# Reordering a four-stage kernel's recurrence turns and their drain, and three repeated products of constants ahead of the experts

## The chip, the core and the metric

One core of a Trainium2 chip. The metric is the device time in microseconds (us), the median of the runs shown. TensorE is PE, VectorE is DVE, ScalarE is ACT, GpSimd is POOL and SyncE is SP.

## What is computed

```python
x = x + L0_attn(layernorm(x))     # two 64x64 states and a gated 64-vector, scanned over 4096 tokens
x = x + L0_ffn(layernorm(x))      # top-2 of 8 experts, 256 -> 1024 -> 256
x = x + L1_attn(x)[0]             # time mixing over tokens, channel mixing
x = x + L1_ffn(x)                 # gated 256 -> 1024 -> 1024 -> 1024 -> 256
```

The first line is where the change lies. For each token, with k, v, q, an importance i, a candidate nu and three shares p:

```python
pred = 0.5 * (q @ fH + q @ sH);  surprise = sigmoid(sum((v - pred)**2))
fH = a_f*fH + (1-a_f)*k(v - k@fH);  sH = a_s*sH + (1-a_s)*[i > 0.5]*k(v - k@sH)
ns = ns + [surprise > 0.7] * 0.1 * (nu - ns)
o  = p0*(q @ fH) + p1*(q @ sH) + p2*ns
```

Then o is scaled by its root mean square, goes through Wo and is added to x; x is normalised, and the router's logits choose two experts per token.

## The kernel before

The 4096 tokens are 32 chunks of 128, and 8 blocks b of four chunks. The recurrence is solved chunk by chunk in 16 **turns** u = 0 to 15 of two chunks each (j = 0, 1). Every engine has its own instruction order, written out by hand in `turn(u)`; semaphores tie them together, and an engine runs its instructions strictly in that order.

Within turn u PE runs eight **levels** n = 0 to 7 for the turn's own two chunks: `level` (lines 1168, 1169) squares the chunk's matrix and (line 1177) multiplies its right side. DVE's `apply(t, p, n)` (line 549) adds each product to the right side, ACT's `square` (lines 911, 914) takes the squares, and level n+1's product waits for `apply` of level n. Between the levels lie three other kinds of work:

- the **tail** for the two chunks of the turn before: PE's `y_transposes` (1185), `y_state` (1195) and `predict` (1201 to 1205), DVE's `rows_w` (556) and `new_state` (563 to 579). `new_state` first makes the new state (563) and then has six small instructions for the outputs (570 to 579, `pp_rdy` at 575);
- the **head** for the two chunks of the next turn: PE's `transposes` (1148, bank 4), ACT's `transposed` (902 to 904), PE's `grams` (1153, bank 4) and DVE's `masks` (535, 538), once for j = 0 around level 4 and once for j = 1 around level 7;
- the **stages of a block** that follow some turns behind: the neuron gates (590), `neuron_steps` and `neurons` (596, the scan at 601), `outputs` (611), `mean_squares` (617), `residual` (629), `stats` and `variances` (636, 641, 643), `norm` (647), ACT's `rows` (957) and `columns` (965), the logits (1229), `choose`, `gates`, `take_ranks` and `places` (662 to 697), and POOL's `scatter` (320), 8 indirect DMAs for a block. `at(u, parity, lag, stage)` runs a stage for block (u - lag)/2 in turns of that parity. Gates, ranks and places begin in turn 7, residuals in turn 4, stages of odd turns at lag 3 in turn 3.

Bank 4 holds the head's transposes and then its grams, for both chunks in turn. So PE's transposes of chunk j = 1 wait until DVE's masks have read the grams of j = 0:

```python
def transposes(t, p, j, bk=4):
    c = t * 2 + j
    pe.wait_ge(kq_rdy, c + 1)
    if c >= 2:
        pe.wait_ge(l_rdy, c)          # counted by masks()
```

They stand behind level 4 and `y_state(·, 1)` on PE; in odd turns `neuron_back` (1220) and the first `z1_columns` (1267) follow, then level 5.

After turn 15 comes the **drain**: the tail of turn 15 and the stages of blocks 5, 6 and 7, again in orders of their own. It ends with the scatters of blocks 6 and 7, 16 indirect DMAs one after another on POOL. Two of them stand ahead of the block end, six behind it. SP then waits for all rows, loads the first 256 rows of expert 0 (1446), PE transposes them (1516), DVE splits them (1640, 1642), and the experts' products begin (1413 to 1415).

Of the kernel before, what the change touches and what calls it, by code (L numbers as in the profile page):

```python
# [18 lines left out]
NC = S // CH  # L19
# [4 lines left out]
PJ = 3 * DS + 3  # L24
LOGIT = 0.8472978603872034
SQUARES = 5
LEVELS = SQUARES + 3
TT = 256
MIN_TILES = 2
# [45 lines left out]
def build(nc, A):  # L75
# [5 lines left out]
    with ctx:  # L81
# [34 lines left out]
        one_m = sb("one_m", [128, 128])  # L116
# [136 lines left out]
        def pj(o, n=1):  # L253
            return slice(o, o + n * DS)
# [48 lines left out]

        def bank_of(b, item):

            return (bank_behind if b == LAST else bank_in_turns)[item]


        def block_of(u, parity, lag):
# [70 lines left out]
        def _(dve):  # L380
# [175 lines left out]
                V.tensor_tensor(Wb[:, j, :].rearrange("p (m n) -> p m n", m=2), X[:, p, j, 0, :, :],  # L556
                                B[6][:, 256:384].rearrange("p (m n) -> p m n", m=2), ALU.subtract).then_inc(w_rdy, 1)

            def new_state(t, j):
                c = t * 2 + j  # L560
                dve.wait_ge(pp_ps, c + 1)
                for m in range(2):
                    last = V.scalar_tensor_tensor(state[half[m], m, :], state[half[m], m, :], alC[half[m], m:m + 1],
                                                  B[6][half[m], 384 + m * DS:384 + (m + 1) * DS], ALU.mult, ALU.add)
                last.then_inc(f_rdy, 1)

                k_, v_ = PR[:, c, pj(0)], PR[:, c, pj(DS)]
                by = lambda s_: small[:, s_, c:c + 1]
                from_fast, from_slow = B[6][:, 0:DS], B[6][:, DS:2 * DS]
                V.tensor_scalar(k_, from_fast, by(T0), None, ALU.mult).then_inc(po_st, 1)  # L570
                V.scalar_tensor_tensor(v_, from_fast, -0.5, v_, ALU.mult, ALU.add).then_inc(po_st, 1)
                dve.wait_ge(po_st, c * 5 + 1)
                V.scalar_tensor_tensor(k_, from_slow, by(T2), k_, ALU.mult, ALU.add).then_inc(po_st, 1)
                dve.wait_ge(po_st, c * 5 + 2)
                V.scalar_tensor_tensor(v_, from_slow, -0.5, v_, ALU.mult, ALU.add).then_inc(pp_rdy, 1)
                dve.wait_ge(po_st, c * 5 + 3)
                V.scalar_tensor_tensor(k_, Wb[:, j, 0:DS], by(T1), k_, ALU.mult, ALU.add).then_inc(po_st, 1)
                dve.wait_ge(po_st, c * 5 + 4)
                V.scalar_tensor_tensor(k_, Wb[:, j, DS:2 * DS], by(T3), k_, ALU.mult, ALU.add).then_inc(po_st, 1)
                dve.wait_ge(f_rdy, c + 2)  # L580

            def fold_words(t, j):
                c = t * 2 + j
# [120 lines left out]
            def turn(u):  # L704

                t, p, deltas, head, tail = u, u % 2, u < TURNS, u + 1 < TURNS, 1 <= u <= TURNS
                if deltas:
                    apply(t, p, 0)
                    fold_words(t, 0)
                at(u, 0, 6, take_logits)  # L710
                at(u, 0, 6, choose, 0)
                at(u, 1, 7, gates)
                at(u, 1, 7, take_ranks)
                at(u, 1, 5, variances)
                if u == 0:
                    key_sums(LAST - 1)
                    neuron_rows(LAST)
                if deltas:
                    apply(t, p, 1)
                if u == 0:  # L720
                    importance(LAST)
                    key_sums(LAST)
                    dve.sem_inc(sq_rdy, 1)
                if tail:
                    rows_w(t - 1, 1 - p, 0)
                at(u, 0, 4, out_scale)
                at(u, 0, 6, choose, 1)
                at(u, 1, 3, neuron_steps)
                at(u, 1, 5, norm)
                if deltas:  # L730
                    apply(t, p, 2)
                if u == 0:
                    share_differences()
                if tail:
                    new_state(t - 1, 0)
                if deltas:
                    apply(t, p, 3)
                if head:
                    masks(t + 1, 1 - p, 0)
                at(u, 0, 4, residual, 0)  # L740
                at(u, 1, 3, neurons)
                at(u, 1, 7, places)
                if deltas:
                    apply(t, p, 4)
                if tail:
                    rows_w(t - 1, 1 - p, 1)
                at(u, 0, 4, residual, 1)
                at(u, 1, 3, outputs)
                if deltas:
                    apply(t, p, 5)  # L750
                if tail:
                    new_state(t - 1, 1)
                if deltas:
                    apply(t, p, 6)
                if head:
                    masks(t + 1, 1 - p, 1)
                if u == 0:
                    token_weights()
                if deltas:
                    apply(t, p, 7)  # L760
                    dve.wait_ge(ap_rdy, (t + 1) * (2 * LEVELS))
                    fold_words(t, 1)
                at(u, 0, 2, neuron_gates)
                at(u, 0, 4, stats)
                at(u, 1, 3, mean_squares)

            go(V.tensor_scalar(seen[:, 0, 0, :], iota8[:, 0, :], float(S // 128), None, ALU.mult))
# [15 lines left out]
            residual(b6, 1)  # L783
            neuron_steps(b7)
            neurons(b7)
            gates(b5)
            take_ranks(b5)
            places(b5)
            outputs(b7)
            stats(b6)  # L790
            mean_squares(b7)
            variances(b6)
            out_scale(b7)
            norm(b6)
            residual(b7, 0)
            residual(b7, 1)
            stats(b7)
# [8 lines left out]
            take_logits(b7)  # L806
            choose(b7, 0)
            choose(b7, 1)
            take_ranks(b7)
            gates(b7)  # L810
            places(b7)

            dve.wait_ge(rk_ps, NB + 1)
# [13 lines left out]
        def _(act):  # L827
# [226 lines left out]
            decays(b7)  # L1054
            A_.activation(sc8[:, 5:6], sc8[:, 3:4], ACT.Sqrt)
            o_squares(b7)
            out_root(b7)
            out_columns(b7)
            norm_root(b6)
            for h in range(2):  # L1060
                rows(b6, h)
            norm_root(b7)
            columns(b6, 0)
            columns(b6, 1)
            for h in range(2):
                rows(b7, h)
            for k in range(KT):
# [6 lines left out]
        def _(pe):  # L1074
# [184 lines left out]

            def z1_columns(b, k):  # L1260
                pe.wait_ge(z1_rdy, 2 * b + 2)
                if k == 1 and b < LAST:
                    pe.wait_ge(z1T_rdy, 2 * b + 1)
                elif 1 <= b < LAST:
                    pe.wait_ge(rk_tk, b)
# [73 lines left out]
            o_columns(b6)  # L1339
            y_state(t, 0)  # L1340
            predict(t, t % 2, 0)
            output(b6)
            y_state(t, 1)
            predict(t, t % 2, 1)
            gate_columns(b7)
            ranks(b5)
            neuron_back(b7)
# [57 lines left out]
        rg_tk, g_st, yb_rdy, to_rdy = sem("raw_gates_taken"), sem("gate_steps"), sem("y_with_bias"), sem("token_rows_ready")  # L1405
        turn_seen = sem("scatter_turns_seen")
        b2_ld = sem("down_biases_loaded")
        wh_rdy, w2_rdy = sem("weights_high"), sem("w2_split")
        p_st2, x_st, h_st = sem("weights_hi_done"), sem("rows_hi_done"), sem("h_hi_done")

# [60 lines left out]
        def _(pool):  # L1471
            go = Steps(pool, p_st2)

            scatter(pool, LAST, 2, 2 * CPB)

            def time_mix_weights():
                pool.wait_ge(wt_ld, 32)
# [28 lines left out]
        def _(pe):  # L1506
# [47 lines left out]
                        pe.drain().then_inc(ex_done, 1)  # L1554

            pe.sem_inc(hs_free, 3)
            rows_T(0)
            expert_tiles(pe, step)
            down(NE - 1, tile_count(pe))
# [1318 lines left out]
```

## Time and profile before

| | |
|---|---|
| time, median of 3 runs | 2117.74 us (2117.61 to 2119.97) |
| the profiled execution: its own time, its span | 2109.22 us, 2107.5 us |
| PE, DVE, ACT, POOL busy | 1907.0, 1357.6, 963.3, 247.8 us |
| mean granted TensorE clock | 0.955 |

The profiled execution took 8.5 us less than the median of the runs; a difference between two kernels is read from the trace and added to the median. Times in the rows are microseconds from the first instruction. The turns run from 112 to 460 us, the drain from 460 to 511 us, the experts' first rows arrive at 528 us. A busy PE is not PE at its peak. A bracket at the end of a timeline row gives the idle time before the instruction and who ended it.

### The profile page before, as it was taken

How to read it: one execution, taken by the hardware profiler on the slowest of the kernel's cores; microseconds unless marked ns; L12 is line 12 of the kernel's file. 1: busy time of each engine (PE TensorE's matmuls, PEld its weight loads, DVE VectorE, ACT ScalarE, POOL GpSimd, SP SyncE). 2: the span in 40 equal slices, each digit the busy share in tenths (PEclk: the TensorE clock that was granted, in tenths of full speed). 3: DMA queues.
4: the chain of work that ended last, by engine and by line, in shares of the span. 5: the costliest groups of instructions: out<-in, count | busy, mean ns of one | idle time of the engine just before them, and what ended most of it. 6: DMA issues, size and time to landing. Idle time of an engine off the chain costs nothing. (4 is left out here: it accounts for less than half of the span.)

```text
span 2107.5 us, 31872 instructions
## 1 busy us (share of the span) xinstructions
PE 1907.0 (90%) x11154; PEld 1617.0 (77%) x11154; DVE 1357.6 (64%) x2810; ACT 963.3 (46%) x1801; POOL 247.8 (12%) x229
## 2 busy tenths in 40 slices
PE   8999999983999999996777589998999999999999
PEld 5788888872899999994445357776888888888887
DVE  7567788774666666665999878884444445345342
ACT  4656666643444444435888555542323232232221
POOL 0000012334233232331000000000000000000000
PEclk9999999995999999998888789999999999999999
DMA  3299411323544332233223413413000000000000
GB/s 105 72 364 408 149 49 59 113 84 106 144 106 88 81 85 47 41 46 110 70 60 90 97 44 120 160 51 139 1 21 20 0 20 9 11 20 0 20 11 11
DMA packets 86146, 170.32 MB, mean 81 GB/s; under 512 B 7264, under 2 KB 49888, under 8 KB 85856
## 3 DMA queue, kind: packets, MB, share of 16 engines
q1 hardware_dynamic: 65968, 132.47, 18.0%
q0 software_dynamic: 18176, 33.70, 8.1%
q10 hardware_dynamic: 1888, 2.67, 0.4%
q8 instruction: 66, 1.08, 0.2%
q14 instruction: 48, 0.39, 0.1%
HBM read 91.61 MB, written 88.74 MB: 86 GB/s over the span
## 5 line engine op out<-in xcount | busy, mean ns | idle before, releaser
L2690 ACT ACTIVATE x_tok<-bank,scl 128x512 f32<-128x512 f32 x128 | 88.3, 690 | 360.2 <-PE bank L2741 359.4
L2740 PE MATMUL bank<-hAh,ffn_h 128*128 128x512 f32 x512 | 202.7, 396 | 0.7 <-DVE x_tok L2617 0.7
L2740 PE MATMUL bank<-hBh,ffn_h 128*128 128x512 f32 x512 | 201.7, 394 | 0.0
L2741 PE MATMUL bank<-hAl,ffn_h 128*128 128x512 f32 x512 | 199.4, 389 | 0.0
L2741 PE MATMUL bank<-hBl,ffn_h 128*128 128x512 f32 x512 | 199.3, 389 | 0.0
L1487 POOL DMA_INDIRECT tokens_behind_spare_rows<-yg,row_of_token x70 | 129.5, 1850 | 302.7 <-DVE row_of_token L1655 283.1
L1590 ACT ACTIVATE h<-bank,b1s 128x256 f32<-128x256 f32 x280 | 124.8, 472 | 31.9 <-PE bank L1415 19.8
L2598 DVE CAST hBh<-x_tok 128x1024 fp32r<-128x1024 f32 x48 | 33.3, 693 | 157.6 <-ACT x_tok L2690 157.0
L2598 DVE CAST hAh<-x_tok 128x1024 fp32r<-128x1024 f32 x48 | 33.3, 693 | 148.7 <-ACT x_tok L2690 148.2
L911 ACT ACTIVATE L<-bank 128x512 f32<-128x512 f32 x128 | 75.4, 595 | 106.1 <-PE bank L1169 105.9
L1177 PE MATMUL bank<-st,L 128*128 128x128 f32 x768 | 116.3, 278 | 6.3 <-DVE st L549 6.2
L1169 PE MATMUL bank<-L 128*128 128x128 f32 x640 | 119.2, 276 | 0.0
L2740 PEld LDWEIGHTS bank<-hAh,ffn_h 128*128 128x128 f32 x512 | 96.1, 188 | 22.8 <-ACTq L2693 1.4
L2741 PEld LDWEIGHTS bank<-hAl,ffn_h 128*128 128x128 f32 x512 | 96.1, 188 | 21.7 <-issue 1.9
L2741 PEld LDWEIGHTS bank<-hBl,ffn_h 128*128 128x128 f32 x512 | 96.1, 188 | 21.3 <-issue 1.4
L2740 PEld LDWEIGHTS bank<-hBh,ffn_h 128*128 128x128 f32 x512 | 96.1, 188 | 21.3 <-ACTq L2693 1.4
L1576 ACT ACTIVATE yg<-yt,own_gates 128x256 f32<-128x256 f32 x68 | 30.8, 500 | 174.5 <-DVE yt L1650 174.5
L549 DVE TENSOR_TENSOR st<-st,bank 128x256 f32<-128x256 f32 x192 | 76.0, 417 | 50.2 <-PE bank L1177 49.2
L1177 PEld LDWEIGHTS bank<-st,L 128*128 128x128 f32 x768 | 100.7, 193 | 8.1 <-ACT L L914 3.8
L2740 PE MATMUL bank<-fTh,ffn_w 128*128 128x512 f32 x256 | 101.2, 395 | 5.1 <-issue 5.1
L1168 PE MATMUL bank<-L 128*128 128x128 f32 x512 | 101.3, 280 | 3.4 <-ACT L L911 3.4
L2741 PE MATMUL bank<-fTl,ffn_w 128*128 128x512 f32 x256 | 101.0, 395 | 0.0
(447 smaller groups left out, 5498.6 us busy)
## 6 DMA issues: line engine op xcount, KB each, us to landing
z_by_expert<-zero SPq DMA_DIRECT2D x64, 520.0 KB, 16.0
ckb<-in_ffn_dram POOLq DMA_DIRECT2D x32, 352.0 KB, 3.5
xg<-z_by_expert SPq DMA_DIRECT2D x36, 260.0 KB, 3.3
x_tok<-in_w_dram SPq DMA_DIRECT2D x8, 1024.0 KB, 7.7
ffn_h<-ffn_copy SPq DMA_DIRECT2D x2, 4096.0 KB, 14.9
x_tok<-after_time_mix SPq DMA_DIRECT2D x15, 512.0 KB, 7.5
st<-in_w_dram SPq DMA_DIRECT2D x6, 1024.0 KB, 7.3
x_tok<-x_T SPq DMA_DIRECT2D x9, 512.0 KB, 4.2
```

Source lines behind the costliest of these rows:

```text
L549: V.tensor_tensor(z_ if SQUARES <= n < LEVELS - 1 else x_, x_, B[2 + j][:, 0:256], ALU.subtract if n == 0 else ALU.add).then_inc(ap_rdy, 1)
L911: A_.activation(L[:, p, j, (n + 1) % 2, :, :], src, ACT.Copy).then_inc(sq_cp, 1)
L1168: T.matmul(B[j][:, 256 * m:256 * m + 128], b_, a, start=True, stop=True)
L1169: last = T.matmul(B[j][:, 256 * m + 128:256 * m + 256], a, b_, start=True, stop=True)
L1177: last = T.matmul(B[2 + j][:, 0:256].rearrange("p (a m d) -> p a m d", a=2, m=2)[:, :, m, :], Ln[:, 2 * m + 1, :], right, start=True, stop ...
L1487: pool.indirect_dma_start(x2_d, bass.IndirectOffsetOnAxis(to_row[:, j:j + 1].bitcast(u32), 0), yg[:, j, :], None, compute_op=ALU.add).then ...
L1576: nc.scalar.activation(yg[:, j, :], yt[:, j, :], ACT.Copy, scale=own_g[:, 0, 0, j:j + 1]).then_inc(y_rdy, 1)
L1590: nc.scalar.activation(h32[:, m, :], B[m % 4][:, 0:TT], ACT.Gelu_apprx_tanh, bias=b1s[:, e * KH + m:e * KH + m + 1]).then_inc(h_act, 1)
L2598: go(V.tensor_copy(dst[0][:, m:m + 2, :], src))
L2690: A_.activation(gq[:, m % 4, :], B[2 + m % 4][:, :], ACT.Gelu, scale=scl[:, off[nm] + m:off[nm] + m + 1]).then_inc(g_act, 1)
L2740: T.matmul(out, w, x[0], start=first, stop=False)
L2741: return T.matmul(out, w, x[1], start=False, stop=last)
```

## The change

Six edits:

1. In the turns, DVE's `new_state` is cut in two. `next_state` (line 563) stays; the six output instructions (`partial_outputs`) run behind the next `apply`: for j = 0 behind `apply` 3, for j = 1 behind `apply` 7 (so behind `apply` 6 and the masks of j = 1 too).
2. In odd turns the scan `neurons` stands ahead of `masks(·, 0)` instead of behind.
3. `variances` moves from the odd turn's start to the end of the even turn before it.
4. In the drain DVE's, ACT's and PE's orders change: the statistics of block 6 come ahead of block 5's gates and places; ACT does block 7's columns, block 6's root, rows and columns ahead of block 7's root; PE's `output(b6)` comes behind `predict(t, ·, 1)`; the last block's gates come ahead of its ranks.
5. Block 6's normalised rows are transposed into banks 7 and 6 instead of 7 twice, so the second four transposes no longer wait for ACT's copy of the first.
6. When POOL has issued its last scatter, PE runs three products of a 128x128 matrix of ones with 512 columns of ones into bank 7, ahead of the first rows' transposes.

```diff
-            return (bank_behind if b == LAST else bank_in_turns)[item]
+            return (7, 6) if (b, item) == (LAST - 1, "z") else (bank_behind if b == LAST else bank_in_turns)[item]
...
+            def new_state(t, j):
+                next_state(t, j)
+                partial_outputs(t, j)
...
                 at(u, 1, 7, take_ranks)
-                at(u, 1, 5, variances)
...
                 if tail:
-                    new_state(t - 1, 0)
+                    next_state(t - 1, 0)
                 if deltas:
                     apply(t, p, 3)
+                if tail:
+                    partial_outputs(t - 1, 0)
+                at(u, 1, 3, neurons)
                 if head:
                     masks(t + 1, 1 - p, 0)
                 at(u, 0, 4, residual, 0)
-                at(u, 1, 3, neurons)
                 at(u, 1, 7, places)
...
                 if tail:
-                    new_state(t - 1, 1)
+                    next_state(t - 1, 1)
                 if deltas:
                     apply(t, p, 6)
...
                 if deltas:
                     apply(t, p, 7)
+                if tail:
+                    partial_outputs(t - 1, 1)
+                if deltas:
                     dve.wait_ge(ap_rdy, (t + 1) * (2 * LEVELS))
                     fold_words(t, 1)
                 at(u, 0, 2, neuron_gates)
                 at(u, 0, 4, stats)
+                at(u, 0, 4, variances)
                 at(u, 1, 3, mean_squares)
...
             neurons(b7)
+            stats(b6)
+            outputs(b7)
+            take_ranks(b5)
+            variances(b6)
+            mean_squares(b7)
+            norm(b6)
             gates(b5)
-            take_ranks(b5)
             places(b5)
-            outputs(b7)
-            stats(b6)
-            mean_squares(b7)
-            variances(b6)
             out_scale(b7)
-            norm(b6)
...
             choose(b7, 1)
+            gates(b7)
             take_ranks(b7)
-            gates(b7)
             places(b7)
...
-            out_root(b7)
             out_columns(b7)
             norm_root(b6)
+            out_root(b7)
             for h in range(2):
                 rows(b6, h)
-            norm_root(b7)
             columns(b6, 0)
             columns(b6, 1)
+            norm_root(b7)
...
-                if k == 1 and b < LAST:
+                if k == 1 and b == LAST - 1:
+                    pe.wait_ge(pp_rdy, NC + 1)
+                elif k == 1 and b < LAST:
                     pe.wait_ge(z1T_rdy, 2 * b + 1)
...
-            output(b6)
             y_state(t, 1)
             predict(t, t % 2, 1)
+            output(b6)
...
             scatter(pool, LAST, 2, 2 * CPB)
+            pool.sem_inc(rows_sent, 1)
...
+            pe.wait_ge(rows_sent, 1)
+            for _ in range(WARM):
+                nc.tensor.matmul(B[7][:, :], one_m[:, :], one_m[:, 0:1].broadcast_to([128, 512]), start=True, stop=True)
             rows_T(0)
```

`WARM` is 3.

## Rows read from the trace of the kernel before

**Rows 1.** Windows: turns 13 and 14; us, then each engine's busy us.

```profile
389.67:413.32 23.65, 22.27 (x189) 21.03 (x187) 19.73 (x69) 16.34 (x43) 6.03 (x8) 1.00 0.41 142
413.32:437.64 24.32, 23.09 (x195) 21.36 (x193) 19.06 (x69) 13.56 (x38) 6.07 (x8) 1.00 0.23 74
```

**Rows 2.** Waits of PE in the turns, 112 to 460 us: total, times, longest.

```profile
PE bank L1177 <- DVE partial_sums L549: 9.1, 15, 1.0
...
PE bank L1168 <- ACT L L911: 3.4, 5, 0.8
```

**Rows 3.** Timeline, turn 14, VectorE: start us, us, then the instruction.

```profile
430.00 0.75 DVE L535 TENSOR_TENSOR L<-bank,maskL 128x256 f32<-128x256 f32 x2
...
431.00 0.87 DVE L629 SCALAR_TENSOR_TENSOR x_tok<-bank,small,x_tok 128x256 f32<-128x256 f32 x2
...
435.01 0.28 DVE L570 TENSOR_SCALAR PR<-bank,small 128x64 f32<-128x64 f32 x1
...
436.18 0.75 DVE L549 TENSOR_TENSOR partial_sums<-st,bank 128x256 f32<-128x256 f32 x2
```

**Rows 4.** Timeline, turn 14, TensorE.

```profile
431.25 0.39 PE L1195 MATMUL bank<-state,YT 128*128 128x128 f32 x2
431.47 0.38 PE L1148 MATMUL bank<-ident,st 128*128 128x128 f32 x2
432.34 1.13 PE L1177 MATMUL bank<-st,L 128*128 128x128 f32 x8 [0.49 <-DVE st L549]
```

**Rows 5.** Timeline, turn 13, TensorE.

```profile
394.51 0.61 PE L1177 MATMUL bank<-st,L 128*128 128x128 f32 x4
...
397.29 0.49 PE L1168 MATMUL bank<-L 128*128 128x128 f32 x2 [0.61 <-ACT L L911]
...
406.30 0.38 PE L1148 MATMUL bank<-ident,st 128*128 128x128 f32 x2
407.14 0.66 PE L1220 MATMUL bank<-ident,nsT 128*128 128x128 f32 x4 [0.47 <-DVE nsT L601]
```

**Rows 6.** Timeline, turn 13, VectorE.

```profile
393.41 0.75 DVE L549 TENSOR_TENSOR st<-st,bank 128x256 f32<-128x256 f32 x2
...
395.93 0.37 DVE L641 BATCH_NORM_AGGREGATE mv<-st 128x2 f32<-128x6 f32 x4
...
396.42 0.75 DVE L549 TENSOR_TENSOR st<-st,bank 128x256 f32<-128x256 f32 x2
...
404.83 0.75 DVE L535 TENSOR_TENSOR L<-bank,maskL 128x256 f32<-128x256 f32 x2
...
405.82 1.27 DVE L601 TENSOR_TENSOR_SCAN nsT<-big,nsT 64x512 f32<-64x512 f32 x1
```

**Rows 7.** Timeline, drain and first rows of the experts, all engines.

```profile
479.96 0.69 PE L1238 MATMUL bank<-ident,big 128*128 128x128 f32 x2 [1.24 <-DVE big L611]
...
483.11 2.07 ACT L957 ACTIVATE Z<-x_tok,small 128x256 f32<-128x256 f32 x4 [0.51 <-DVE small L648]
...
485.24 1.11 PE L1267 MATMUL bank<-ident,Z 128*128 128x128 f32 x4 [0.71 <-ACT Z L957]
...
488.30 0.20 ACT L952 ACTIVATE small<-small 128x4 f32<-128x4 f32 x1 [3.12 <-DVE small L643]
...
489.13 1.09 PE L1267 MATMUL bank<-ident,Z 128*128 128x128 f32 x4 [2.79 <-ACT zT L965]
...
500.57 0.97 POOL L320 DMA_INDIRECT z_by_expert<-Z,slotz  x1 [11.27 <-DVE slotz L697]
...
521.10 0.97 POOL L320 DMA_INDIRECT z_by_expert<-Z,slotz  x1 [0.30 <-issue]
...
528.15 1.12 PE L1516 MATMUL bank<-ident,xg 128*128 128x128 f32 x4 [19.87 <-DMA xg<-z_by_expert]
```

**Rows 8.** Timeline, TensorE, first expert tile.

```profile
530.94 0.58 PE L1413 MATMUL bank<-xTh,w_0h 128*128 128x256 f32 x1 [1.67 <-DVE xTl L1642]
...
536.86 0.32 PE L1413 MATMUL bank<-xTh,w_0h 128*128 128x256 f32 x1
```

**Rows 9.** Windows in the drain; the last three columns are PEclk, DMA share, GB/s.

```profile
470.35:472.09 1.74, 0.00 (x1) 0.00 (x0) 1.52 (x9) 0.00 (x0) 0.00 (x0) 1.00 0.48 64
472.09:473.78 1.69, 0.00 (x0) 0.00 (x1) 1.58 (x9) 0.42 (x1) 0.00 (x0) 0.50 0.86 349
```

**Rows 10.** The chain that ended last: two products of 512 columns.

```profile
1465.22 1.72 PE bank L2724 x4
```

## The prediction on record

> **What bounds the kernel now.** I read the windows of two typical turns first. PE is busy 22.27 of turn 13's 23.65 us and 23.09 of turn 14's 24.32 us, all at the full clock; DVE 19.7 and 19.1 [rows 1]. So a turn is PE's work plus PE's few waits, and DVE has 4 to 5 us to spare, but not everywhere. The waits of PE say where it waits: 15 times, 9.1 us in all, for DVE's `apply` 6 ahead of level 7, and 5 times, 3.4 us, for ACT's squares [rows 2]. Then I read both kinds of turn in order of time, PE against DVE, asking at each place of the change what DVE has just done and what PE wants of it next. Last I read the drain: there PE is mostly idle, and the end is set by a chain: block 6's normalised rows, their transposes, logits, choice, places, then 16 scatters on POOL from 500.57 to 522.07 without a pause, the landing, the load, the transposes at 528.15 [rows 7]. After that the stages follow one another, and a shift of the drain's end passes on whole.
>
> Back-to-back PE instructions overlap: one of 0.39 us is followed after 0.22 [rows 4]. A wait therefore costs its idle time and some 0.15 us of lost overlap.
>
> **Edit 1, the gain.** Outputs of chunk j = 1 take DVE 1.17 us (435.01 to 436.18) between the new state and `apply` 6, and level 7 waits for that `apply` [rows 3]. Without them `apply` 6 is ready when PE arrives. All the waits go: 9.1 + 15 x 0.15 = 11.3 us [rows 2]. That is 0.9 us in an even turn and in the early ones, 0.45 in odd turns from 5 on, where PE has transposes of its own ahead of level 7.
>
> **Edits 1 and 2, what they put in the way.** The outputs of j = 0 move behind `apply` 3. Before, they lay in DVE's idle time ahead of `apply` 3; now the masks of j = 0 stand behind them, and PE's transposes of j = 1 wait for these masks, because the bank is the same.
> - Even turns. Masks start at 430.00 and end at 431.08, and PE's transposes start at 431.47 [rows 3, 4]: 0.4 us of slack against 1.17 of delay. Worse, `residual` (431.00) and `apply` 4 follow in DVE's order, and level 5 at 432.34 already waits for that `apply` (0.49 us) [rows 3, 4]. So level 5 is later by the whole 1.17. Less the 0.90 won at level 7: +0.27 for each of turns 4, 6, ..., 14. Turn 2 has no residual: about 0.
> - Odd turns. The masks start at 404.83 [rows 6]. Now the outputs (1.17) and the scan (1.27, 1.30 with its issue) stand ahead: start at 407.30, end 1.08 later at 408.38. PE's transposes stood at 406.30 [rows 5], now 408.4: +2.1. What is won is the wait of `neuron_back` for the scan, 0.47 + 0.15 [rows 5], since it now comes behind a later transpose. Net +1.5. `apply` 4 is ready by then and costs nothing more.
>
> **Edits 1 and 3 at the odd turn's start.** Turn 13 begins at 389.67, `apply` 0 starts 3.74 us into it [rows 6], and level 1's first product 4.84 us into it [rows 5]: 0.7 us of slack once the half of `apply` 0 (0.42) is done. In front of `apply` 0 now also stand the outputs of j = 1 (1.17) and `variances` (395.93 to 396.42, 0.49 [rows 6]), and `apply` 7 is itself 0.05 later: 1.71 more, product at 5.9 instead of 4.84, +1.1. What goes in return is PE's wait for the squares (0.61 + 0.15 at 397.29 [rows 5]): ACT was late there since its root for the block waited for `variances`. It occurs in the five odd turns from 7 on [rows 2]. Net +0.3 there. Turn 5 had no such wait, and no ranks (0.36 us of PE) to cover: +1.4. Even turns have room: their `apply` 0 stands ahead of 2 us of logits on PE.
>
> **Sum of the turns.** Turns 7, 9, 11, 13: 0.3 + 1.5 - 0.45 = 1.35, together 5.4. Turn 5: 1.4 + 1.5 - 0.45 = 2.45. Turn 3 (no residual, statistics or first z transposes): 1.6 - 0.9 = 0.7. Turn 15 has no masks; its scan comes 1.17 later, its wait at level 7, the longest, 1.0 and 0.15 [rows 2], goes: +0.4 with the start's 0.3. Six even turns: 1.6. Turns 0 to 2: 0. Total **+10.6 us**. DVE is not the bound in busy time; it becomes one at two places of each turn.
>
> **Edits 4 and 5, the drain.** The outputs of turn 14's second chunk now stand ahead of block 5's logits on DVE: +1.17. `output(b6)` behind `predict` gives back 0.4. Then the chain of block 6: o_columns ends at 480.65 [rows 7]. ACT now takes block 7's columns at once, then block 6's root (its variance is ready at 480.6, since gates and places no longer stand ahead), and rows start at about 481.8 instead of 483.11: -1.3. The first four transposes end 1.1 us after they start at 485.24, and the second four stood at 489.13, waiting 2.79 us for ACT's copy, which was behind a root at 488.30 [rows 7]. In another bank they follow at once at 486.3: -2.9. Together -4.2; logits, choice and places of block 6 follow unchanged. Block 5's places come some 4 us later, but POOL has 11.27 us of idle time there [rows 7]. Block 7's slots must come within 10.2 us of block 6's; they shift with it and gain 0.8 more by the gates. Drain: 1.2 - 0.4 - 4.2 = **-3.4 us**.
>
> **Edit 6, the products.** Two products of 512 columns took 1.72 us at the full clock [rows 10], so three take 2.6, or 5.2 at half. They start when POOL's last issue ends (522.07) and rows arrive at 528.15 [rows 7]: they end at 527.3 and delay nothing (0.9 us of cover; if the release came late, up to 1 us more). What they can give is the clock. The experts' first products run from 530.94 at half speed; at 536.86 they turn fast (0.58 against 0.32 us) [rows 8]. 5.9 us at half speed is 2.95 us to win at most. But the clock must survive the pause: in the drain it was granted whole while PE stood idle from 470.35 and was halved at 472.09 [rows 9]. From 527.3 to 530.94 PE does 0.6 to 1.1 us of transposes and nothing else. And it took 5.9 us of dense work to raise it [rows 8], where the products last 5.2. I take **0**, and keep -2.95 as the bound. The Trainium skill's page "TensorE: Matmul & The Clock Gate" (section "Why this matters for your kernels") advises keeping TensorE busy and warming up with matmuls first (the Trainium skill, that is, speaks for this edit); by that rule the whole 2.95 would be won, and the time would be 2121.9. No row here shows a warmed-up start; the nearest shows a clock lost in a pause.
>
> **Result.** +10.6 - 3.4 + 0 = +7.2 us. The profiled execution would go from 2109.2 to 2116.4; the median from 2117.7 to **2124.9**.
>
> **Bounds.** The slack figures are good to some 0.1 us each, at two stalls in each of 13 turns: turns +8 to +13. The drain's gain may be 2.5 to 5; the clock 0 to 2.95. Low 8 - 5 - 2.95 = 0 (2117.8), high 13 - 2.5 = +10.5 (2128.2).
>
> **Rivals.**
> - The clock stays whole into the experts: 2124.9 - 2.95 = 2121.9. For it: the first tile's end is PE's, so the gain passes on; against it [rows 9]. 15%.
> - The odd turns cost half (ACT or PE has slack that I don't see, or the scan's early end helps more): the turns +5, 2119.3. 15%.
> - Faster: the late masks are hidden. If PE's transposes have over 2 us of room, only the gain at level 7 stays: -11.3 + 1.1 x 5 at the odd starts less their 3.4 + 5 x 0.15 of waits gone, about -10 for the turns, -3.4 for the drain: 2104.3. It decides at 1.2 us of slack between the masks' end and the transposes in even turns, 2.5 in odd ones; turn 14 shows 0.39 [rows 3, 4], which is why I give it 10%.
> - The drain's shift stops at POOL or at the block end, since clearing semaphores and splitting expert 0's weights don't move: the gain of 4.2 is lost, 2129. These ended at 520, 8 us before they were wanted. 7%.
>
> The forecast has 53%. A measurement of this kernel tells about 0.2% (4.2 us) from no change. Slower by more (over 2122): most of the forecast, all of the lost drain, half of the clock's rival: 0.60. Within: the rest of these and the half-cost rival: 0.27. Faster: 0.13. For 8 in 10 the range takes in the rivals at 2119.3 and 2121.9 and noise on both sides of the bounds, and leaves the hidden masks out: 2113 to 2130.
>
> **What would show it.** In the waits of PE, the 9.1 us for `partial_sums` (line 549) should be gone, and new idle time of about 2 us in odd turns should stand ahead of line 1148, released by the masks, and about 0.8 in even turns; line 1177 should wait over 1 us for `apply` 0 in odd turns from 5. The wait for ACT's squares should be gone. An odd turn should last 25.0 instead of 23.65 us, an even one 24.6. In the drain the eight z transposes should run as one group, and the first scatter of block 6 come 4 us earlier counted from turn 15's last level. The first expert products should still be slow for some us. The prediction is wrong above all if the transposes don't wait for the masks, or if another wait at level 5 hid them.

## The result and the profile after

The changed kernel takes 2133.78 us (median of 4 runs, 2129.56 to 2134.72) against 2117.68 (4 runs) before, a ratio of 1.0070 [1.0052, 1.0087]: 16.1 us slower. Two more measurements beside the kernel before agree with it in direction: 1.0058 for the same kernel again, 1.0068 for it without edit 6. The forecast was 2124.9, at most 2130. The direction was right, the size less than half of what came.

The profiled execution took 2134.72 us (span 2133.0); its busy line of TensorE, from the page:

```profile
PE 1925.4 (90%) x11160; PEld 1630.9 (76%) x11160; DVE 1359.4 (64%) x2810; ACT 963.5 (45%) x1801; POOL 248.0 (12%) x229
```

PE is busy 18.4 us longer than the 1907.0 us before, of which the three products are 5.5 (below), and the mean granted clock is 0.952 instead of 0.955. So not all of the loss is waiting: PE also worked more slowly somewhere. Windows of turn 13 and turn 14, as in [rows 1]:

```profile
405.77:432.59 26.82, 24.28 (x188) 22.76 (x187) 20.16 (x71) 17.71 (x47) 6.04 (x8) 0.94 0.36 126
432.59:457.06 24.47, 23.02 (x194) 21.47 (x193) 19.08 (x68) 13.72 (x39) 6.72 (x8) 1.00 0.23 74
```

Turn 14 went from 24.32 to 24.47 us, turn 13 from 23.65 to 26.82 (the odd turns 5 to 11 take 26.53 or 26.54). In turn 13 PE is busy 24.28 us instead of 22.27, for the same work, and the clock column, 1.00 before [rows 1], is 0.94. The waits of PE in the turns:

```profile
PE bank L1160 <- DVE QM L539: 18.4, 14, 2.1
PE bank L1189 <- DVE st L550: 10.4, 14, 3.3
...
PE bank L1232 <- DVE nsT L608: 0.9, 1, 0.9
...
PE bank L1189 <- DVE partial_sums L550: 0.7, 1, 0.7
```

Line 1160 is `transposes`, 539 `masks`, 1189 a level's product, 550 `apply`, 1232 `neuron_back`. The 9.1 us in 15 waits for `partial_sums` [rows 2] have become 0.7 in one, and the waits for ACT's squares [rows 2] are gone. In their place PE waits 14 times for the masks, 2.0 or 2.1 us in each of the six odd turns 3 to 13 and 0.75 in the others. The longest, in turn 13, in order of time; first TensorE, whose rows answer to [rows 5]:

```profile
422.73 0.39 PE L1207 MATMUL bank<-state,YT 128*128 128x128 f32 x2
425.18 0.41 PE L1160 MATMUL bank<-ident,st 128*128 128x128 f32 x2 [2.06 <-DVE QM L539]
425.42 0.68 PE L1232 MATMUL bank<-ident,nsT 128*128 128x128 f32 x4
425.89 1.06 PE L1281 MATMUL bank<-ident,Z 128*128 128x128 f32 x4
426.75 1.92 PE L1189 MATMUL bank<-st,L 128*128 128x128 f32 x8
```

and VectorE in the same stretch, which answers to [rows 6]:

```profile
421.14 0.42 DVE L550 TENSOR_TENSOR st<-st,bank 128x256 f32<-128x256 f32 x1 [0.92 <-PE bank L1189]
421.48 0.28 DVE L573 TENSOR_SCALAR PR<-bank,small 128x64 f32<-128x64 f32 x1
...
422.64 1.27 DVE L608 TENSOR_TENSOR_SCAN nsT<-big,nsT 64x512 f32<-64x512 f32 x1
423.94 0.76 DVE L536 TENSOR_TENSOR L<-bank,maskL 128x256 f32<-128x256 f32 x2
424.62 0.41 DVE L539 TENSOR_TENSOR QM<-bank,maskQ 128x256 f32<-128x256 f32 x1
```

The outputs (421.48), the scan (422.64) and only then the masks (423.94 to 425.03): the queue that edits 1 and 2 made, and behind it a pause of PE of 2.06 us. Behind the pause comes what I had not priced. The level's group of eight products takes 1.92 us at 426.75; the same group takes 1.06 to 1.13 elsewhere. Three windows that meet at the clock's edges (last three columns: granted clock, DMA share, GB/s):

```profile
422.40:425.81 3.41, 1.34 (x13) 1.18 (x12) 3.31 (x10) 0.65 (x3) 0.00 (x0) 1.00 0.00 0
425.81:429.22 3.41, 3.41 (x19) 3.41 (x17) 2.09 (x8) 2.75 (x10) 0.00 (x0) 0.50 0.00 0
429.22:432.64 3.42, 3.42 (x28) 3.11 (x28) 2.49 (x8) 2.59 (x10) 0.00 (x0) 1.00 0.00 0
```

PE is busy 1.34 of the first 3.41 us; then the clock is granted at half for 3.41 us, in which PE gets through 19 matmuls with no pause, where the next stretch at the whole clock holds 28. The trace has such a stretch at 221.0, 272.2, 323.4, 374.6 and 425.8 us, in the five turns 5, 7, 9, 11 and 13, and at no other place from 120 to 480 us. In the trace of before the clock is whole from 120 to 450 us:

```profile
120.00:450.00 330.00, 312.80 (x2613) 293.10 (x2612) 258.43 (x882) 209.06 (x571) 59.02 (x86) 1.00 0.47 174
```

The drain, all engines, answering to [rows 7]:

```profile
506.44 0.69 PE L1250 MATMUL bank<-ident,big 128*128 128x128 f32 x2 [1.22 <-DVE big L618]
...
510.22 1.97 PE L1281 MATMUL bank<-ident,Z 128*128 128x128 f32 x8 [0.53 <-ACT Z L969]
512.87 3.58 PE L1241 MATMUL bank<-small_weights,zT 128*128 128x8 f32 x16 [0.69 <-ACT zT L977]
...
536.21 5.49 PE L1576 MATMUL bank<-one_m 128*128 128x512 f32 x6 [5.04 <-POOLq L1490]
...
544.69 0.97 POOL L321 DMA_INDIRECT z_by_expert<-Z,slotz  x1 [0.30 <-issue]
...
551.40 1.12 PE L1532 MATMUL bank<-ident,xg 128*128 128x128 f32 x4 [9.70 <-DMA xg<-z_by_expert]
```

The eight z transposes run as one group, without a wait between them. From block 6's `o_columns` (506.44) to its logits (512.87) it is 6.43 us. Before it was 10.95, from 479.96 [rows 7] to

```profile
490.91 3.58 PE L1229 MATMUL bank<-small_weights,zT 128*128 128x8 f32 x16 [0.69 <-ACT zT L965]
```

so 4.5 us are won. The three products (each is recorded as two) run from 536.21 to 541.70 at half speed, released while POOL still had seven scatters to issue, and PE is idle 9.70 us behind them. Right behind them the clock is whole, but only while PE does nothing, and it is half again before the rows arrive:

```profile
541.87:545.28 3.41, 0.00 (x0) 0.00 (x0) 0.00 (x0) 0.00 (x0) 2.54 (x3) 1.00 0.32 116
545.28:551.40 6.12, 0.00 (x1) 0.01 (x1) 0.00 (x0) 0.86 (x1) 0.38 (x1) 0.50 0.29 85
```

The shown traces of before and after are 25.5 us apart in span, the medians 16.1. The profiled execution of after has waits in turn 15 and the drain that before's has not. They go with the chip and not with the order of the instructions (last section). Below, sizes in turn 15 and the drain are read between traces that are free of them.

### The profile page after: what moved, and what is told of

It reads as the page before. It is cut to its first block and busy times, and to the rows that moved or that the text cites. A ratio compares the mean times of both kernels' runs of the same rounds, so it can differ in the third digit from the quotient of the medians.

```text
span 2133.0 us, 31878 instructions
## 1 busy us (share of the span) xinstructions
PE 1925.4 (90%) x11160; PEld 1630.9 (76%) x11160; DVE 1359.4 (64%) x2810; ACT 963.5 (45%) x1801; POOL 248.0 (12%) x229
## 3 DMA queue, kind: packets, MB, share of 16 engines
q8 instruction: 66, 1.08, 0.2%
## 5 line engine op out<-in xcount | busy, mean ns | idle before, releaser
L1189 PE MATMUL bank<-st,L 128*128 128x128 f32 x768 | 121.3, 286 | 10.6 <-DVE st L550 10.4
```

Of the source, the lines that this page charges most:

```text
L1189: last = T.matmul(B[2 + j][:, 0:256].rearrange("p (a m d) -> p a m d", a=2, m=2)[:, :, m, :], Ln[:, 2 * m + 1, :], right, start=True, stop ...
```

## The experiments

All measured ratios are to the kernel before, run on the same chip beside it. The lengths of turns 1 to 14 are taken from one `y_transposes` to the next, in one profiled execution of each kernel:

| kernel | odd turns 5 to 13 | even turns 6 to 14 | half clock in them | ratio |
|---|---|---|---|---|
| before | 22.58 (turn 5), 23.65 to 23.74 | 24.31 to 24.33 | none | 1 |
| after | 26.53 to 26.54, turn 13 26.82 | 24.47 | 5 times 3.4 us | 1.0070 |
| `scan_late` | 24.48 | 24.47 | none | 1.0026 |
| `filled_pause` | 24.89 | 24.48 | none | 1.0029 |
| `turns_back` | as before | as before | none | 0.9982 |
| `masks_early` | 23.33 | 23.32 | none | 0.9937 |

**The turns alone.** Edits 1 to 3 in the kernel before; drain and products as they were.

> The kernel before with VectorE's turn order alone changed (edits 1 to 3); drain, banks and products as before. Theory A (the turns cost all of it: PE's transposes wait for the masks, 18.4 us in the waits after, and these pauses halve the clock five times for 3.4 us, another 8.5 us lost): 2117.7 + 18 in the turns + 1.2 at the drain's start, about 2137. The clock falls to one half once in each of about five odd turns. Rival B (the turns cost the 7 to 10 us that I forecast and the rest came in the drain): 2125 to 2128, with the clock whole in the turns.

Measured: 2127.57 us against 2108.52, 1.0089 [1.0072, 1.0106], +19.1 us. The turns are the whole loss and more: from the first `y_transposes` to the last, which opens the drain, it is 18.2 us longer, with a stretch at half clock in each of the same five turns. From the drain's `y_transposes` to block 6's first scatter it is 40.28 us instead of 39.14: +1.14, the 1.17 of outputs that the forecast had put ahead of block 5's logits.

**The turns back.** The changed kernel with DVE's `turn` as in before; edits 4 to 6 stay.

> The changed kernel with VectorE's turn order as before; drain, banks and products as changed (edits 4 to 6). Theory A: the drain's chain is 4.6 us shorter as its rows showed (rows 1.5 earlier, transposes 2.8 earlier), products worth nothing: about 2113. Rival C (the waits that the trace after shows in the drain without a releaser, on VectorE and ScalarE, belong to the new order): 2117 to 2119, no gain.

Measured: 2104.89 us against 2108.52, 0.9982 [0.9973, 0.9992], 3.6 us faster than before. From the drain's `y_transposes` to block 6's first scatter it is 33.56 us instead of 39.14, 5.6 less: 1.1 ahead of block 6's `o_columns` and 4.5 from there to its logits. That is more than the medians show; their interval reaches from 1.7 to 5.7 us.

**The masks early.** The changed kernel; of edit 1 only the half for chunk 1 (j = 1) is kept, and edit 2 is undone:

```diff
                 if tail:
-                    next_state(t - 1, 0)
+                    new_state(t - 1, 0)
                 if deltas:
                     apply(t, p, 3)
-                if tail:
-                    partial_outputs(t - 1, 0)
-                at(u, 1, 3, neurons)
                 if head:
                     masks(t + 1, 1 - p, 0)
                 at(u, 0, 4, residual, 0)
+                at(u, 1, 3, neurons)
```

> The changed kernel with the outputs of chunk 0 ahead of apply 3 and the scan behind the masks again; the outputs of chunk 1 stay behind apply 7, variances stay at the even turn's end. Theory A (the late masks are the cost): no wait of PE for the masks, no halved clock, the 9.1 us of waits ahead of level 7 still gone: turns about 8 us shorter than before, drain 3.4 shorter, 2106. Rival D (the late apply 0 in odd turns halves the clock by itself): clock halved in some odd turns, 2112 to 2118.

Measured: 2096.18 us, 0.9937 [0.9921, 0.9954], 12.3 us faster than before and some 27 faster than the changed order (`no_products`, below, +14.5 on the same chip). A second measurement on another chip:

> masks_early once more, beside products_13_2 on one chip: 11 to 12 us below the kernel before (2096 against 2108.5 at first).

Measured: 2094.11 against 2109.31, 0.9934 [0.9920, 0.9947], -15.2 us. This order is the best of those tried, and close to the change. In its turns PE's waits, read in the second measurement's trace, have no masks and no `partial_sums` among them:

```profile
PE bank L1187 <- DVE st L550: 6.7, 13, 1.4
PE bank L1230 <- DVE nsT L608: 2.7, 6, 0.5
PE bank L1224 <- DVE small L598: 0.6, 3, 0.2
```

An even turn gains 1.0 us over before, about the 0.9 that the forecast gave for level 7. So chunk 1's half of edit 1 is good, and chunk 0's half and edit 2 together made the loss.

**Without the products.** `WARM = 0`.

> The changed kernel without the three products of ones; PE's wait for POOL's count stays. Theory A: the products run 9.7 us before the rows land, as POOL's queue releases them seven issues early, and the clock falls again: worth nothing, 2133.8 within 1.5. Rival E (they raise the clock at the wrong time and so put off the next rise: after them it stayed halved for 17 us): 2 us faster, 2131 to 2132.

Measured: 2123.04 against 2108.52, 1.0068 [1.0048, 1.0089], +14.5 us. The changed kernel again, on another chip:

> The changed kernel itself beside the others on one chip. Theory A (products worth nothing): within 1.5 us of no_products, so 14.5 us above the kernel before. If the waits without a releaser in turn 15 and the drain of its first trace (some 7 us) belong to the program, they show again and it is 7 us slower than no_products; if they were of that execution or chip, they don't.

Measured: 2132.52 against 2118.73, 1.0058 [1.0041, 1.0074], +13.8 us. Between them no effect of the products can be told; the intervals, some 4 us to either side, would hide one of 2 us. The drain, read in the trace without them, takes 35.41 us from its `y_transposes` to block 6's first scatter, 3.7 less than before; the first rows' transposes come 14.7 us later than before's 528.15 [rows 7]:

```profile
542.84 1.09 PE L1532 MATMUL bank<-ident,xg 128*128 128x128 f32 x4 [19.46 <-DMA xg<-z_by_expert]
545.59 0.58 PE L1428 MATMUL bank<-xTh,w_0h 128*128 128x256 f32 x1 [1.67 <-DVE xTl L1662]
```

**The scan late.** At this point two theories stood: that the odd turns lose what DVE's queue ahead of the masks loses (outputs and scan, some 2.4 us), or that something at half clock behind the pause takes a part of its own. This kernel undoes edit 2 alone:

```diff
                 if tail:
                     partial_outputs(t - 1, 0)
-                at(u, 1, 3, neurons)
                 if head:
                     masks(t + 1, 1 - p, 0)
                 at(u, 0, 4, residual, 0)
+                at(u, 1, 3, neurons)
                 at(u, 1, 7, places)
```

> The changed kernel with the scan (neurons) behind the masks and the residual again (edit 2 undone, all else as changed). Theory A (each delay of the masks is paid by PE, and the length of the pauses in a turn decides whether the clock is halved): PE's wait for the masks in odd turns falls from 2.1 to about 0.8 us, so 6 turns x 1.3 less, neuron_back then waits some 1.8 for the scan, since that comes later still; the sum of the pauses in an odd turn stays and so do the halved clocks: within 3 us of the changed kernel. Rival F (the one long pause of 2.1 us is what halves the clock): the halved stretches go, 8 to 10 us faster than the changed kernel.

Measured: 2124.79 against 2118.73, 1.0026 [1.0014, 1.0037], +6.1 us. Against +13.8 for the changed kernel on the same chip, more than half of the loss goes with the scan alone. The longest wait for the masks is 0.8 us instead of 2.1, no stretch in turns 2 to 14 has half clock, and an odd turn lasts 24.48 instead of 26.53 us. That is 2.05 us for an instruction that takes 1.3 with its issue and whose early place saves `neuron_back` a wait of 0.47 [rows 5]: the queue alone can't account for it. The theory put first, by which the sum of the pauses in a turn decides the clock and the time stays within 3 us, has failed; its rival, the one long pause, had 8 to 10 us against 7.7 measured.

This kernel and `masks_early` differ only in chunk 0's half of edit 1. An odd turn is 24.48 us here and 23.33 there, an even one 24.47 and 23.32: the outputs ahead of the masks, 1.17 us of VectorE, cost 1.15 us in every turn, without any fall of the clock.

**The pause filled.** The direct test of the clock: the changed kernel, in odd turns from 3 on with two products of ones into bank 7 ahead of the transposes that wait.

```diff
                     if head:
+                        if n == 4 and u % 2 and u >= 3:
+                            for _ in range(2):
+                                T.matmul(B[7][:, :], one_m[:, :], one_m[:, 0:1].broadcast_to([128, 512]), start=True, stop=True)
                         if n in (0, 4):
                             transposes(t + 1, 1 - p, n // 4)
```

DVE's order, and so the moment at which the masks are ready, stays as in the change; only what PE does meanwhile differs.

> The changed kernel, with two more products of ones (512 columns, 1.7 us at the full clock) on PE in odd turns from 3 on, just ahead of the transposes that wait for the masks; bank 7 is free there. They change no wait of anyone else. Theory A2 (formed after scan_late: PE's 2.1 us pause for the masks is paid twice, as itself and as a stretch of 3.4 us at half clock, 1.5 us each in five to six odd turns): with PE busy through the pause the clock stays whole, an odd turn lasts 25.0 instead of 26.5 us, and the kernel is 7.5 us faster than the changed one: 7 us above the kernel before where the changed one is 14.5 above. Rival (the clock is lost to the stall at level 1, or to something else than idle time): the halved stretches stay, no faster.

Measured: 2114.47 against 2109.31, 1.0029 [1.0020, 1.0039], +5.2 us, where +7 was expected. TensorE in turn 13, which compares with 422.73 and 425.18 of the changed kernel:

```profile
414.47 0.39 PE L1207 MATMUL bank<-state,YT 128*128 128x128 f32 x2
414.69 1.89 PE L1309 MATMUL bank<-one_m 128*128 128x512 f32 x4
416.92 0.41 PE L1160 MATMUL bank<-ident,st 128*128 128x128 f32 x2 [0.34 <-DVE QM L539]
417.17 0.60 PE L1232 MATMUL bank<-ident,nsT 128*128 128x128 f32 x4
```

The transposes stand 2.45 us behind line 1207 in both kernels: the masks are ready at the same moment, and the products take no time of their own. Behind it the whole turn takes 24.89 us instead of 26.5. The clock (the third number from the end) is whole over the turns:

```profile
120.00:450.00 330.00, 315.04 (x2560) 289.20 (x2559) 250.75 (x850) 201.89 (x560) 53.24 (x76) 1.00 0.46 170
```

1.64 us in each of five turns, 8.2 us in all, is the price of the half clock alone; half of 3.4 us is 1.7. The changed kernel by itself agrees. In the trace of `after_again`, turn 13 has the same pause of 2.06 us, and the clock stays whole behind it:

```profile
424.50:427.90 3.40, 3.40 (x31) 3.40 (x32) 2.89 (x12) 2.94 (x11) 0.00 (x0) 1.00 0.00 0
```

That turn takes 24.88 us, as with the pause filled.

**The variances back.** `masks_early` with edit 3 undone.

> As masks_early, with variances in the odd turn again: of the turn edits only the outputs of chunk 1 behind apply 7 are left. By the rows: apply 0 in odd turns 0.49 us earlier, so PE's stall at level 1 shrinks from about 1.1 to 0.6 in turns 5 to 13, but PE's wait for ScalarE's squares (3.4 us in 5 waits, 4.2 with lost overlap) comes back, partly: 1 to 2 us slower than masks_early, 2097 to 2098 where the kernel before takes 2108.5. Rival: the stall at level 1 is the costlier, 1 us faster.

Measured: 2109.31 against 2118.73, 0.9953 [0.9937, 0.9970]. Turns 7, 9, 11 and 13 take 24.20 to 24.35 us instead of 23.33, about 0.9 more each, and turn 5, which had no wait for the squares before, 23.15, 0.2 less: 3.6 us by the trace. `masks_early` stood at 0.9937, which makes 3.4 us of difference, in ratios whose intervals overlap; 1 to 2 was expected. Edit 3 was good too.

**One bank.** `turns_back` with edit 5 undone: block 6's z transposes go to bank 7 twice.

```diff
-            return (7, 6) if (b, item) == (LAST - 1, "z") else (bank_behind if b == LAST else bank_in_turns)[item]
+            return (bank_behind if b == LAST else bank_in_turns)[item]
...
-                if k == 1 and b == LAST - 1:
-                    pe.wait_ge(pp_rdy, NC + 1)
-                elif k == 1 and b < LAST:
+                if k == 1 and b < LAST:
                     pe.wait_ge(z1T_rdy, 2 * b + 1)
```

> turns_back (turns as before, drain's orders and products as changed) with block 6's z transposes in bank 7 twice again (edit 5 undone). The second four then wait for ScalarE's copy of the first, which is no longer behind block 7's root: 0.6 of copy, 1.1 of transposes less overlap, about 1.4 us later than in turns_back. So 2.2 us below the kernel before where turns_back was 3.6 below: most of the 2.9 that I gave to the bank belongs to ScalarE's order. Rival: the bank is worth 2.9 by itself, 0.7 below.

Measured: 2104.57 against 2109.31, 0.9977 [0.9967, 0.9986], 4.7 us faster than before; both expectations, 2.2 and 0.7, are missed. Beside 0.9982 for `turns_back` (on another chip) there is, in time, no effect that can be told. In the trace there is one:

```profile
485.32 1.12 PE L1274 MATMUL bank<-ident,Z 128*128 128x128 f32 x4 [0.53 <-ACT Z L964]
487.21 1.09 PE L1274 MATMUL bank<-ident,Z 128*128 128x128 f32 x4 [0.78 <-ACT zT L972]
488.99 3.58 PE L1236 MATMUL bank<-small_weights,zT 128*128 128x8 f32 x16 [0.69 <-ACT zT L972]
```

From the first transpose to the logits it is 3.67 us, and 2.65 with two banks (`turns_back`). So the bank is worth 1.0 us of chain once ACT's root stands elsewhere; the 2.79 us of wait before [rows 7] were mostly the root ahead of the copy. That 1.0 is below what the two ratios can tell apart.

**Thirteen products.** `masks_early` with `WARM = 13`, so that PE is busy until the rows land.

> As masks_early with 13 products of ones for 3, so that PE is busy from POOL's early release (13.9 us ahead of the rows) until the rows land: 13 x 0.86 at the full clock plus 1.7 to 3.4 us for its slow start is 12.9 to 14.5 us. Theory A (the three were worth nothing because 9 us of idle time followed): now the clock is whole when the experts' products begin, the first tile takes 2.5 to 3 us less, less up to 0.6 of delay of the rows' transposes: 2 to 3 us faster than masks_early. Rival G (the transposes and the pause for the split let the clock fall anyway): no faster.

> masks_early with 13 products for 3, on the same chip as masks_early_2. Theory A: whole clock at the experts' start, 1 to 3 us faster than masks_early_2 if the first products start within some 2 us of the rows' transposes. Rival G: the clock falls in the pause for the split anyway, as it did at 526.6 in the first trace: no difference beyond 1 us.

Measured: 2103.95 against 2118.73, 0.9923 [0.9907, 0.9940], and 2095.52 against 2109.31, 0.9934 [0.9920, 0.9947]; with three products 0.9937 and 0.9934. The second one's TensorE at the experts' start, which answers to [rows 8]:

```profile
496.15 14.22 PE L1574 MATMUL bank<-one_m 128*128 128x512 f32 x26 [5.04 <-POOLq L1488]
512.59 0.66 PE L1530 MATMUL bank<-ident,xg 128*128 128x128 f32 x4 [2.21 <-DMA xg<-z_by_expert]
514.91 0.38 PE L1426 MATMUL bank<-xTh,w_0h 128*128 128x256 f32 x1 [1.67 <-DVE xTl L1660]
...
515.53 0.42 PE L1427 MATMUL bank<-xTl,w_0h 128*128 128x256 f32 x1
```

Now the transposes take 0.66 instead of 1.12 us [rows 7] and the first expert products run fast. From the fifth on they take 0.41 or 0.42 again: the clock is halved at 515.4 for 3.4 us, behind a stretch in which PE did 0.66 us of transposes between waits of 2.21 and 1.67 us. With three products, in `masks_early_2`, it was half until 520.9, from 517.31 on 3.6 us of experts at half speed. The whole clock is there at the start and gone a moment later, for about as long. In the first trace (`products_13`) the wait for the split was 4.62 us, the clock was halved within it, and no expert product ran fast at the start:

```profile
523.14:526.60 3.46, 0.66 (x4) 0.42 (x4) 2.02 (x1) 3.46 (x3) 0.00 (x0) 1.00 0.84 247
526.64:530.00 3.36, 1.58 (x7) 1.59 (x8) 3.33 (x6) 1.43 (x1) 0.00 (x0) 0.50 0.38 98
```

## Why the prediction came out as it did

- **Edit 1, the gain at level 7.** Right: 9.1 us in 15 waits became 0.7 in one; `masks_early` shows it by itself, 1.0 us for an even turn.
- **The masks late, and with them the transposes.** Right in place and size: PE waits 2.06 us at line 1160 in odd turns, where "+2.1" was forecast, and 0.75 or so in the other turns.
- **Even turns, +0.27.** Measured +0.16 (24.31 to 24.47).
- **The odd turn's start.** Right: the first product behind the late `apply` 0 stands at 411.63, 5.86 us into turn 13, where 5.9 was forecast and 4.84 was before, and the wait for ACT's squares is gone. Only 0.34 us of the 1.0 shows as a wait for `apply`; the squares ahead of it are later as well.
- **Sum of the turns: "Turns 7, 9, 11, 13: 0.3 + 1.5 - 0.45 = 1.35".** Here the prediction failed, by the rule that it used for every pause: "A wait therefore costs its idle time and some 0.15 us of lost overlap." The rule holds where the clock stays whole. (The 0.39 us of [rows 4] that it was read from is a pair of instructions; the overlap of 0.17 us is right.) With the pause filled an odd turn lasts 24.89 us, 1.2 more than before, where 1.35 was forecast; turn 5 went from 22.58 to 24.89, +2.3, where 2.45 was forecast. The 14 lengths from turn 1's `y_transposes` to turn 15's sum to 334.93 us with the pause filled and to 325.18 before: +9.8 us, against 10.2 of the forecast's 10.6 (the rest was turn 15's). The sum is closer than its terms, since turn 3's miss and the even turns' cancel. What is missing is a term, put at nothing without a reason: behind a pause of 2.1 us PE also did its work at half clock for 3.4 us, which cost 1.64 us in each of five turns, 8.2 us. With it the forecast would have been 2133.1. I had used [rows 9] against the products, a clock lost while PE stood idle, and had not asked the same of the 2.1 us pause that I was adding in each of six odd turns.
- **Turn 3.** 21.99 to 23.35, +1.4 for the 0.7 forecast. Its wait at line 1160 is 2.00 us, and its clock stayed whole in this execution. The further 0.7 stays unexplained.
- **Edits 4 and 5, the drain.** -3.7 measured (`no_products`), -3.4 forecast: +0.7 ahead of block 6's `o_columns` (1.2 - 0.4 forecast), -4.5 from there to the logits (-4.2 forecast), +0.1 behind them. But "-1.3" and "-2.9" were shared out wrongly: from `o_columns` to logits 4.5 us are won, 3.5 of them by ACT's order (10.95 to 7.44 in `one_bank`) and 1.0 by the bank, not 1.3 and 2.9.
- **Edit 6.** 0 forecast, and nothing measured that is clear of noise. But the way there was another. The products do not start at the end of POOL's last issue: they start 8.5 us before it begins, with seven scatters still to come in the trace. Their 5.5 us were followed by a whole clock (541.87), which the prediction had doubted, and it was lost while PE stood idle for 9.70 us ahead of the rows. Where thirteen products reached up to the rows, the pauses for the rows and the split took it, and these are the pauses that the prediction had named. The Trainium skill's page "TensorE: Matmul & The Clock Gate" (section "Why this matters for your kernels"), by which the 2.95 us would have been won, is borne out by `products_13_2` for the first four expert products only, and by `products_13` for none.
- **The rivals.** Hidden masks were excluded by the 14 waits. The odd turns did not cost half: 1.2 us with the pause filled, of 1.35. The clock did not stay whole into the experts: it was half from 545.28 on, and the rows came at 551.40. The drain's shift did pass on: the first rows are 14.7 us later in `no_products` (+18.8 at the drain's `y_transposes`, -3.7 to block 6's first scatter, -0.4 behind it), and its median is 14.5 higher.

The whole: turns 1 to 14 +18.3 in the trace of after (9.8 as stalls, 8.2 behind them at half clock, and 0.3 more in turn 13), drain -3.7, products 0: +14.6, where +14.5, +13.8 and +16.1 were measured.

## What to carry to other kernels

Before work is moved on an engine that is not the bound, list what now stands behind it and who waits for that; here 1.17 us of outputs and 1.3 of scan ahead of 1.08 us of masks cost more than the whole of the change's gain. A stall in the middle of dense TensorE work is to be priced twice: its own time, and whether the granted clock survives it. Windows laid over the place, with their clock column, show it at once, and a few products without use in the pause show which part is which.

## What the runs showed of the hardware

- **The same pause, with and without a fall of the clock.** Four traces have the changed order in the turns (`after`, `after_again`, `turns_only`, `no_products`), each with six pauses of 2.00 to 2.07 us at line 1160. Behind 21 of these 24 the clock was half for 3.4 us, behind three it stayed whole: in turn 3 of `after` and of `turns_only`, and in turn 13 of `after_again`. Turn 3's pause was 2.00 us in all four. In the trace of `after` the turn took 23.35 us; in the trace of `no_products`, with the same order, the clock was half from 173.1 us on for 3.4 us, and the turn took 24.97. Both pauses, each in two windows (up to the end of the pause, and behind it): after,

```profile
170.40:174.40 4.00, 2.00 (x19) 1.83 (x18) 3.93 (x13) 0.77 (x2) 0.00 (x0) 1.00 1.02 406
174.40:177.80 3.40, 3.40 (x31) 3.27 (x29) 2.92 (x12) 3.20 (x13) 0.00 (x0) 1.00 1.03 407
```

and `no_products`:

```profile
169.00:173.10 4.10, 2.10 (x19) 1.93 (x19) 3.79 (x11) 1.03 (x3) 0.00 (x0) 0.99 1.02 405
173.10:176.50 3.40, 3.40 (x18) 3.40 (x17) 1.95 (x8) 2.32 (x10) 0.00 (x0) 0.51 1.04 407
```

  31 matmuls against 18 in 3.40 us, 1.62 us of turn. So a pause of 2.0 us can go either way, which by itself would spread the runs of one kernel by 1.6 us for each such pause. What decides it, no run here shows. The waits of 0.75 us for the masks in the turns of `scan_late` had no fall behind them in turns 2 to 14.
- **POOL's count comes ahead of its scatters in the trace.** The count placed behind the 16th scatter released PE at 536.21, while the last scatter stands at 544.69. No run tells whether the queue runs ahead or the issues are recorded late.
- **One kernel, two kinds of ending.** In the profiled executions where the kernel before takes 2118 us (the result's own and those of chip 15) DVE and ACT show waits in turn 15 and the drain without an engine that releases them ("remote"), and turn 15 lasts 27 instead of 21 us; on the other two chips (2108.5 and 2109.3 us) there is none, in any kernel. The kernel before has its trace from the faster kind alone. ACT's splitting of expert 0's weights comes late on the former too. The waits of ACT behind the turns, in the changed kernel:

```profile
ACT w_0h L1588 <- issue: 22.4, 1, 22.4
```

and in `no_products`, on a chip of the other kind:

```profile
ACT w_0h L1588 <- issue: 10.0, 1, 10.0
```

In the first, DVE's second weight split and with it the first expert products were held up (PE waits 3.89 us for `xTl`, not 1.67). No run here takes these waits apart, so their cause stays open. The ratio of the change is the same on either kind within the noise (1.0058 and 1.0070; 1.0068 for `no_products`), so the explanation above doesn't rest on them.
